# A decoder layer on one core: LN1's turned rows made by GpSimd, one transposition for a sequence's shifts, and a new order of all steps

## The chip, the cores and the metric

The kernel runs on one core of one Trainium2 chip. The metric is the device time of one execution in microseconds (us), lower is better. The time before is the median of three runs, 1078.32 us (1075.54 to 1079.03).

## What is computed

The input x is 32 sequences of 128 tokens by 256 features in f32; `ctx_1024` has the same shape. The layer has three parts, each with a residual (LN is layer normalisation without weights, eps 1e-5):

```
x = x + attn(LN1(x))        # causal linear attention, 16 heads of 16, phi = elu + 1, biases bq, bk, bv, bo
x = x + xattn(LN2(x), ctx)  # softmax attention on ctx, 16 heads of 16, Wq, Wk, Wv
x = x + ffn(LN3(x))         # silu(x w1) * (x w2), 256 -> 1024; gelu(h1), gelu(h2), 1024 -> 1024; w3, 1024 -> 256
```

The feed-forward weights are ternary, each with a scale per output.

## The kernel before, in words

**Tiles.** A group g (0 to 15) is two sequences, 256 tokens. Attention works on groups. The feed-forward net works on turns f (0 to 7) of two groups, 512 tokens. Activations that enter a matmul as f32r are split in two parts, the rounded value and the rest, and both are multiplied, so each feed-forward matrix costs two matmuls per 128x128 tile: 2816 matmuls of 128x512 in all, lines L1232 (`gate`), L1247 (`hidden`) and L1267 (`w3`).

**A group's attention, in the order of its data.** `load_x` brings x with tokens on partitions into `x_in` (L587). `ln1_stats` takes mean and variance on DVE (L861, L864) and the reciprocal deviation on POOL (L698, L701). `ln1` normalises in place on DVE (L867). `ln1T` turns the two sequences with four transpositions on PE (L1050, helper `turn`), and ACT (L756) and DVE (L871) take the rounded part and the rest out of PSUM into `xn1T`. Then q, k and v (L1074, L1079, L1089), the linear attention in 32-wide tiles (L1132 `scores`, L1105 `add_up`), the projection (L1182, L1185), LN2 (its transpositions are L1050 too, with `xb`), `xq`, and `max`: a first pass of the cross attention's scores, from which DVE takes each head's maximum (L981). `shift` writes minus the maximum as a bf16 pair into `nshift` (L990, L992), PE turns it with four bf16 transpositions per sequence (L1204), and ACT copies the 128x512 result to `shiftT` (L812). `x_scores` begins with matmuls of `onesb` and `shiftT` over 2 rows (L1125), which put the shift into PSUM, and adds the scores (L1132); `x_exp` (L816), `x_sums`, `x_div` and `x_turn` follow, then LN3, whose normalised rows are turned on PE (L1050, `xn`) into `hidden_b`. LN3's mean and deviation are stored to DRAM (`keep_stats`, L666), read back to all partitions (`load_stats`, L670), and POOL rebuilds the residual from them with four 128x256 operations a group (L722).

**Kept keys and values.** For groups 1 to 14 `xk` and `xv` are computed ahead of time, stored (`keep_k`, `keep_v`) and read back when their group comes (`load_k`, `load_v`).

**Weights.** `copy_weights` copies the 24 feed-forward weight tiles to `weights_scratch`, issued from ACT (L833). `ring` loads them tile by tile into a ring of four, 24 loads a turn (L613). `load_bits` and `low_bits` look at the low bits of the original weights.

**What sets the order.** At build time a planner (L62 to L391, with `LEAD`, `AT`, `needs` and `PATIENCE`) writes a fixed list of steps for each of the five engines. Each step has a due time (`PITCH` of 61.5 us times the group, plus an offset per step, plus a `LEAD` per engine and step), a booked duration, and the steps that it needs. On every engine the step with the earliest due time among those ready is put next. On PE, steps in 32-wide tiles wait until they are `PATIENCE` old or three of them have gathered, while feed-forward work fills in. The engines then run their lists strictly in order, with semaphores between them. SP's list holds nearly all DMAs; a wait on SP holds up every DMA behind it in the list. `x_in` is a single buffer: `load_x(g)` waits until PE has turned group g - 1.

## Time and profile before

| | |
|---|---|
| median of three runs | 1078.32 us |
| lowest, highest | 1075.54, 1079.03 us |
| span of the profiled execution | 1076.9 us |
| own time of the profiled execution, apart from its span | not given |
| TensorE busy, matmuls | 97%, 9898 |
| VectorE, ScalarE, GpSimd busy | 71%, 50%, 24% |
| mean granted TensorE clock | 0.996 |

PE is TensorE's matmuls, PEld its weight loads, DVE VectorE, ACT ScalarE, POOL GpSimd, SP the queue that issues DMAs. L12 is line 12 of the kernel before. A busy time unites overlapping instructions; the ends of matmuls are modelled. A stretch's row gives its limits and length, then for each engine the busy us with the count of instructions, then the granted clock as a share of full speed, the mean busy share of the 16 DMA engines, and GB/s. A group's row has the line, engine, operation, output and inputs, count, busy us and mean ns, and the engine's idle time before it with what ended it. A tile's row has ns min/median/max and the first and last start. A wait's row has total us, times, longest.

### The profile page before, as it was taken

To read this page: it belongs to the slowest core of one execution; us is meant where nothing else is said; L and a number is where in the kernel's file an instruction comes from. 1 tells how busy PE (TensorE), PEld (TensorE's weight loads), DVE (VectorE), ACT (ScalarE), POOL (GpSimd) and SP (SyncE) were. 2 spreads that over 40 slices of the span, in tenths; PEclk is the share of its full clock that TensorE was granted. 3 is DMA by queue.
4 is the path that set the end of the run, shared out by engine and by line. 5 is a ranking of instruction groups with operands and counts; after the bars stand their busy time and mean duration, and the time that the engine had idled before them with its cause. 6 is when DMAs were issued, how large, how long until landed. Compare 5 with 4: busy or idle time off the path is not lost.

```text
span 1076.9 us, 25119 instructions
## 1 busy us (share of the span) xinstructions
PE 1046.7 (97%) x9898; PEld 871.6 (81%) x9898; DVE 769.2 (71%) x1708; ACT 539.0 (50%) x857; POOL 259.7 (24%) x363
## 2 busy tenths in 40 slices
PE   7997899999999999999999999999999999999997
PEld 7987887888778888788887888888878788888886
DVE  6996798777987789888789676978587528433421
ACT  4452454646464644654555555473734364733431
POOL 4322345010531012601044101521026002400500
PEclk9999999999999999999999999999999999999999
DMA  5468887443644346534264434553364436545551
GB/s 163 168 215 276 270 269 245 138 138 113 198 146 138 104 109 206 164 106 149 85 230 142 149 109 137 174 166 109 109 218 149 166 105 206 184 148 178 181 169 65
DMA packets 76742, 174.86 MB, mean 162 GB/s; under 512 B 10960, under 2 KB 26448, under 8 KB 76624
## 3 DMA queue, kind: packets, MB, share of 16 engines
q1 hardware_dynamic: 73168, 161.70, 45.5%
q10 hardware_dynamic: 3456, 11.54, 3.7%
q8 instruction: 81, 1.33, 0.5%
q14 instruction: 37, 0.30, 0.1%
HBM read 145.38 MB, written 39.35 MB: 172 GB/s over the span
## 4 chain that ended last, share of the span: by engine, by line
PE 83%; DVE 8%; DMA 3%; issue 2%; POOL 1%; SPq 1%; ACT 0%; ACTq 0%; DVEq 0%; POOLq 0%
PE bank L1247 42%; PE bank L1132 7%; PE bank L1232 7%; PE bank L1267 5%; PE bank L1105 5%; PE bank L1074 5%; PE bank L1089 3%; PE bank L1079 2%; PE bank L1050 2%; DVE hidden_full L1012 1%; PE bank L1182 1%; DVE mx L981 1%; DMA stats_scratch<-mv 1%; DMA weight_ring<-weights_scratch 1%; PE bank L1125 1%
## 5 line engine op out<-in xcount | busy, mean ns | idle before, releaser
L1247 PE MATMUL bank<-hidden_a,weight_ring 128*128 128x512 f32 x1024 | 249.1, 395 | 0.0
L1247 PE MATMUL bank<-hidden_b,weight_ring 128*128 128x512 f32 x1024 | 247.9, 394 | 0.3 <-DVE inexact_flag L1037 0.3
L1247 PEld LDWEIGHTS bank<-hidden_b,weight_ring 128*128 128x128 f32 x1024 | 187.9, 188 | 39.8 <-issue 1.6
L1247 PEld LDWEIGHTS bank<-hidden_a,weight_ring 128*128 128x128 f32 x1024 | 187.6, 188 | 38.9 <-issue 0.8
L849 ACT ACTIVATE hidden_full<-bank,columns_sb 128x512 f32<-128x512 f32 x128 | 88.2, 689 | 187.9 <-PE bank L1247 187.2
L698 POOL TENSOR_TENSOR ve<-mv,eps 128x1 f32<-128x1 f32 (+1 forms) x80 | 18.5, 231 | 524.6 <-DVE mv L864 524.6
L1232 PE MATMUL bank<-hidden_b,weight_ring 128*128 128x512 f32 x512 | 122.9, 393 | 1.4 <-DMA weight_ring<-weights_scratch 1.0
L1232 PEld LDWEIGHTS bank<-hidden_b,weight_ring 128*128 128x128 f32 x512 | 94.3, 188 | 22.4 <-DMA weight_ring<-weights_scratch 1.8
L737 POOL TENSOR_TENSOR hidden_a<-hidden_full,hidden_a 128x512 fp32r<-128x512 f32 x64 | 83.8, 1313 | 104.2 <-ACT hidden_a L844 103.0
L1020 DVE TENSOR_TENSOR hidden_a<-hidden_full,hidden_a 128x512 fp32r<-128x512 f32 x64 | 43.8, 684 | 76.9 <-ACT hidden_a L855 76.7
L816 ACT ACTIVATE att_x<-bank 128x512 f32<-128x512 f32 x128 | 66.3, 603 | 48.0 <-PE bank L1132 47.9
L981 DVE TENSOR_REDUCE mx<-bank 128x4 f32<-128x512 f32 x128 | 80.4, 678 | 6.7 <-PE bank L1132 6.7
L960 DVE TENSOR_TENSOR att_l<-bank,cst 128x512 f32<-128x512 f32 x128 | 80.6, 679 | 6.2 <-PE bank L1132 6.0
L1020 DVE TENSOR_TENSOR hidden_b<-hidden_full,hidden_b 128x512 fp32r<-128x512 f32 x64 | 47.0, 736 | 51.0 <-ACT hidden_b L855 50.9
L901 DVE STREAM_TRANSPOSE by_token<-bank 128x512 f32<-128x512 f32 x64 | 45.6, 713 | 51.1 <-PE bank L1105 50.9
L839 ACT ACTIVATE hidden_full<-bank,s1h 128x512 f32<-128x512 f32 x64 | 44.0, 687 | 53.3 <-PE bank L1232 51.9
L1267 PE MATMUL bank<-hidden_a,weight_ring 128*128 128x512 f32 x256 | 65.9, 400 | 0.0
L722 POOL TENSOR_TENSOR residual<-residual,stats 128x256 f32<-128x256 f32 x64 | 59.0, 943 | 26.6 <-DMA stats<-stats_scratch 25.3
L844 ACT ACTIVATE hidden_a<-hidden_full 128x512 fp32r<-128x512 f32 x64 | 40.2, 630 | 31.3 <-DVE hidden_full L1015 31.1
L1267 PEld LDWEIGHTS bank<-hidden_a,weight_ring 128*128 128x128 f32 x256 | 45.8, 188 | 9.3 <-issue 0.4
L849 ACT ACT_TABLE_LOAD x39 | 50.0, 1283 | 0.7
L1015 DVE SCALAR_TENSOR_TENSOR hidden_full<-bank,s,hidden_full 128x512 f32<-128x512 f32 x64 | 48.1, 751 | 2.3
(135 smaller groups left out, 1715.5 us busy)
## 6 DMA issues: line engine op xcount, KB each, us to landing
weight_ring<-weights_scratch SPq DMA_DIRECT2D x160, 512.0 KB, 4.0
weights_scratch<-in_h ACTq DMA_DIRECT2D x16, 512.0 KB, 5.2
xn3T_scratch<-hidden_b SPq DMA_DIRECT2D x16, 512.0 KB, 4.2
weight_bits<-in_h SPq DMA_DIRECT2D x32, 256.0 KB, 4.2
weight_ring<-weights_scratch SPq DMA_DIRECT2D x32, 256.0 KB, 2.8
values_scratch<-hidden_full SPq DMA_DIRECT2D x14, 512.0 KB, 4.3
xv<-values_scratch SPq DMA_DIRECT2D x14, 512.0 KB, 4.9
x_in<-in_x SPq DMA_DIRECT2D x16, 256.0 KB, 2.8
```

The source lines that it names most:

```text
L722: last = eng.tensor_tensor(half[:, c], half[:, c], (sd, mean)[n], (ALU.mult, ALU.add)[n])
L737: eng.tensor_tensor(HA[:, 1, n, :], full[:, n % NFULL, :], HA[:, 0, n, :].bitcast(F32), ALU.subtract)\
L816: eng.activation(att_x[:, (NU * g + n) % NX, :, :], pbank("x_scores", g, n)[:, :].rearrange("p (j s) -> p j s", j=4), ACT.Exp, scale=SCALE ...
L849: eng.activation(full[:, (KH + n) % NFULL, :], pbank("hidden", g, n)[:, :], ACT.Gelu, scale=sc).then_inc(h_full, 1)
L960: eng.tensor_tensor(att_l[:, (NU * g + n) % NL, :, :], pbank("lin_scores", g, n)[:, :].rearrange("p (j s) -> p j s", j=4), causal.rearrang ...
L981: eng.tensor_reduce(mx[:, b, 4 * r:4 * r + 4], pbank("max", g, n)[:, :].rearrange("p (j t) -> p j t", j=4), AX.X, ALU.max).then_inc(max_do ...
L1020: eng.tensor_tensor(dst[:, 1, m, :], full[:, (KH + n) % NFULL, :], dst[:, 0, m, :].bitcast(F32), ALU.subtract)\
L1074: eng.matmul(pbank(step, g)[:, m * T:(m + 1) * T], w[:, i, c, m * P:(m + 1) * P], src[:, 0, c, :], start=(c + i == 0), stop=False)
L1132: mm = eng.matmul(pbank(step, g, 4 * b + r)[:, j * S:(j + 1) * S], stationary(rows, e, m, b), moving(rows, e, m, b), start=not shifted, st ...
L1232: mm = eng.matmul(pbank(step, g, n)[:, :], ring[:, n // 4, at_:at_ + P], HB[:, part, kk, :], start=(kk == 0 and part == 0), stop=(kk == C ...
L1247: mm = eng.matmul(pbank(step, g, n)[:, :], ring[:, slot, kk * P:(kk + 1) * P], src[:, part, kk, :], start=(kk == 0 and part == 0), stop=(k ...
L1267: mm = eng.matmul(pbank(step, g, c)[:, :], ring[:, slot, kk % 4 * P:(kk % 4 + 1) * P], HA[:, part, kk, :], start=(kk == 0 and part == 0), ...
```

## The change

1. **LN1 turned.** The host also passes `xT`, x with features on rows. For groups 1 to 15, `x_in` is loaded a second time after the statistics, with turned x (`load_xT`, 256 KB). Means and reciprocal deviations go to DRAM (`keep_stats1`) and come back spread over all partitions in two loads, means first (`load_stats1`, 128 KB each, into one buffer). POOL subtracts and multiplies in place, two 128x256 operations each (`xn1`). ACT and DVE read `xn1T`'s two parts from there. Group 0 stays as it was.
2. **Shifts.** `nshift` packs a sequence's 16 maxima in pairs into one 128x128 bf16 tile, 8 columns of each 32. PE turns it once. ACT writes it four times, each time with another mask as its scale, and the matmuls with ones go over 8 rows.
3. **Order.** New `LEAD` values and an `OFFSET` per group, `PATIENCE` 17.2, copies of the weights from 34.8 us on in steps of 8.76 us, `load_bits` in steps of 13.17 us, and tanh not counted as needing gelu's table. `load_x` waits for `xn1T` (DVE).

```diff
-    SPARE, PATIENCE, HOLD, MANY = 1, 18.5, 0, 3
+    SPARE, PATIENCE, HOLD, MANY = 1, 17.2, 0, 3
+    IN_TURNS = ("keep_xn", "keep_x2", "gate", "hidden", "w3", "tanh", "gated", "gate_round", "gate_rest", "gelu", "gelu_rest",
+                "out", "ring", "copy_weights", "split", "load_bits", "low_bits")
-            tasks[engine, step, g, n] = (rank + t + LEAD.get((engine, step), 0), took[engine])
+            lead = LEAD.get((engine, step), 0) + (0 if step in IN_TURNS else OFFSET[g])
+            tasks[engine, step, g, n] = (rank + t + lead, took[engine])
-    LEAD = {("gpsimd", "bias"): -14.1, ("gpsimd", "ctx"): -18.7, ("gpsimd", "gate_rest"): -4.2, ("gpsimd", "ln1_stats"): -3.1,
+    LEAD = {("gpsimd", "bias"): -14.9, ("gpsimd", "ctx"): -337.4, ("gpsimd", "gate_rest"): -294.4,
...
+    OFFSET = [-49.7, -36.8, 17.6, 63.5, -31.0, 123.6, -12.0, 61.9, 77.8, -63.7, -8.2, 64.3, 145.2, -46.8, -6.9, 115.5]
-        steady("ln1", vector=-12.6, took=dict(vector=.75))
-        steady("ln1T", tensor=-10.5, scalar=-8.63, vector=-7.75, took=dict(tensor=.4, scalar=.52, vector=.6))
+        if g == 0:
+            steady("ln1", vector=-12.6, took=dict(vector=.75))
+            steady("ln1T", tensor=-10.5, scalar=-8.63, vector=-7.75, took=dict(tensor=.4, scalar=.52, vector=.6))
+        else:
+            steady("load_xT", sync=-30, took=dict(sync=5))
+            steady("keep_stats1", sync=-25, took=dict(sync=2.2))
+            for n in range(2):
+                steady("load_stats1", n, sync=-24 + 4 * n, took=dict(sync=3))
+                steady("xn1", n, gpsimd=-20 + 4 * n, took=dict(gpsimd=1.75))
+            steady("ln1T", scalar=-8.63, vector=-7.75, took=dict(scalar=.52, vector=.6))
...
-    GELUS = ("tanh", "gelu")
+    GELUS = ("gelu",)
-    AT |= {("scalar", "copy_weights", j): 62 + 5.4 * j for j in range(NCH)}
-    AT |= {("sync", "load_bits", i, j): 150 + 17.5 * (NWB * i + j) for i in range(8) for j in range(NWB)}
+    AT |= {("scalar", "copy_weights", j): 34.8 + 8.76 * j for j in range(NCH)}
+    AT |= {("sync", "load_bits", i, j): 197.8 + 13.17 * (NWB * i + j) for i in range(8) for j in range(NWB)}
...
-                    wait_count(eng, xn1_turned, g)
+                    if g == 1:
+                        eng.wait_ge(xn1_turned, 1)
+                    elif g > 1:
+                        eng.wait_ge(xn1T_done, g)
...
+                    elif step == "load_xT":
+                        eng.wait_ge(LN1["mean_var"], GB * g + GB)
+                        eng.dma_start(x_t, xT.rearrange("(c p) t -> p c t", p=P)[:, :, T * g:T * g + T]).then_inc(xT_loaded, 16)
+                    elif step == "keep_stats1":
+                        eng.wait_ge(LN1["rstd"], g + 1)
+                        eng.wait_ge(mean1_copied, g)
+                        eng.dma_start(st1_d[g].rearrange("w p b -> p w b"), stats1_out[:, :, :]).then_inc(stats1_stored, 16)
+                    elif step == "load_stats1":
+                        eng.wait_ge(stats1_stored, 16 * g)
+                        if n == 1:
+                            eng.wait_ge(xn1_centred, g)
+                        elif g > 1:
+                            eng.wait_ge(xn1_made, g - 1)
+                        eng.dma_start(stats1[:, :, :].rearrange("p s b -> p (s b)"),
+                                      st1_d[g, n].rearrange("s b -> (s b)").partition_broadcast(P)).then_inc(stats1_loaded, 16)
...
+                        if g:
+                            eng.tensor_copy(stats1_out[:, 0, :], mv[:, 0, :, 0]).then_inc(mean1_copied, 1)
+                    elif step == "xn1":
+                        half = x_t.rearrange("p c (b s) -> p c b s", b=GB)
+                        mean_or_rstd = stats1[:, :, :].rearrange("p s b -> p b s")
+                        if n == 0:
+                            eng.wait_ge(xT_loaded, 16 * g)
+                        eng.wait_ge(stats1_loaded, 32 * g - 16 + 16 * n)
+                        for c in range(C):
+                            last = eng.tensor_tensor(half[:, c], half[:, c], mean_or_rstd, (ALU.subtract, ALU.mult)[n])
+                        last.then_inc((xn1_centred, xn1_made)[n], 1)
...
-                        eng.activation(xn1T[:, 0, :, :], halves(pbank(step, g)), ACT.Copy).then_inc(xn1T_hi, 1)
+                        eng.activation(xn1T[:, 0, :, :], halves(pbank(step, g)) if g == 0 else x_t, ACT.Copy).then_inc(xn1T_hi, 1)
...
-                        eng.activation(shiftT[:, n, :], pbank(step, g, n)[:, 0:2 * S].bitcast(BF16), ACT.Copy).then_inc(sh_done, 1)
+                        for j in range(4):
+                            last = eng.activation(shiftT[:, n, j * S:(j + 1) * S], pbank(step, g, n)[:, 0:S // 2].bitcast(BF16), ACT.Copy,
+                                                  scale=cst[:, 258 + j:259 + j])
+                        last.then_inc(sh_done, 1)
...
-                            eng.matmul(pbank(step, g, 4 * b + r)[:, :], onesb[32 * r:32 * r + 2, :], shiftT[32 * r:32 * r + 2, b, :],
+                            eng.matmul(pbank(step, g, 4 * b + r)[:, :], onesb[32 * r:32 * r + 8, :], shiftT[32 * r:32 * r + 8, b, :],
...
-                        for j in range(4):
-                            mm = eng.transpose(pbank(step, g, n)[:, j * S // 2:(j + 1) * S // 2].bitcast(BF16), nshift[:, n, j, :], identb[:, :])
-                        mm.then_inc(sh_psum, 1)
+                        eng.transpose(pbank(step, g, n)[:, 0:S // 2].bitcast(BF16), nshift[:, n, :], identb[:, :]).then_inc(sh_psum, 1)
```

The rest of the diff replaces every value of `LEAD`, adds the new steps to the table of needs, and adds buffers, semaphores and four mask columns in `constants`. Before it takes a group's statistics, DVE also waits until those of the group before are stored.

## Rows read from the trace of the kernel before

**Rows 1.** The page's head: span, busy time by engine

```profile
span 1076.9 us, 25119 instructions
...
PE 1046.7 (97%) x9898; PEld 871.6 (81%) x9898; DVE 769.2 (71%) x1708; ACT 539.0 (50%) x857; POOL 259.7 (24%) x363
```

**Rows 2.** Stretches: length; PE, PEld, DVE, ACT, POOL busy; clock; DMA share; GB/s

```profile
0.00:144.00 144.00, 126.82 (x1773) 118.05 (x1774) 115.70 (x295) 62.07 (x121) 44.13 (x67) 0.98 0.68 221
20.00:80.00 60.00, 57.19 (x827) 53.03 (x830) 54.06 (x136) 27.25 (x53) 18.32 (x26) 1.00 0.55 184
106.00:144.00 38.00, 35.26 (x511) 32.72 (x512) 30.87 (x80) 16.68 (x34) 11.06 (x18) 0.92 0.83 261
144.00:1004.00 860.00, 853.95 (x7837) 699.64 (x7836) 638.27 (x1391) 454.82 (x702) 204.69 (x285) 1.00 0.48 156
1004.00:1077.00 73.00, 65.89 (x291) 53.90 (x290) 15.27 (x24) 22.09 (x36) 10.88 (x12) 0.98 0.38 127
```

**Rows 3.** Waits of PE from 0 to 144 us: total us, times, longest

```profile
PE bank L1074 <- ACT hidden_full L806: 5.6, 2, 4.5
PE bank L1062 <- ACT identb L744: 5.5, 1, 5.5
```

**Rows 4.** Waits of SP's queue from 84 to 106 us, same columns

```profile
SPq L670 <- DMA stats_scratch<-mv: 9.9, 1, 9.9
```

**Rows 5.** Timeline of PE, 88 to 109 us: start, us, what

```profile
89.46 0.66 PE L1050 MATMUL bank<-cst,xn 128*128 128x128 f32 x4
89.87 0.71 PE L1074 MATMUL bank<-xn1T,wk 128*128 128x256 f32 x4
...
90.64 0.62 PE L1074 MATMUL bank<-xn1T,wk 128*128 128x256 f32 x4
...
95.96 0.40 PE L1204 MATMUL bank<-identb,nshift 128*128 128x128 bf16 x4 [0.33 <-DVE nshift L992]
96.17 0.72 PE L1182 MATMUL bank<-wo,oT 128*128 128x256 f32 x4
...
107.21 1.05 PE L1074 MATMUL bank<-ctxs,xwk 128*128 128x256 f32 x4
```

**Rows 6.** Groups by line: busy us, mean ns, idle before

```profile
L1247 PE MATMUL bank<-hidden_a,weight_ring 128*128 128x512 f32 x1024 | 249.1, 395 | 0.0
...
L1204 PE MATMUL bank<-identb,nshift 128*128 128x128 bf16 x128 | 12.9, 225 | 2.9 <-DVE nshift L992 2.9
...
L1050 PE MATMUL bank<-cst,x_in 128*128 128x128 f32 x64 | 10.2, 283 | 0.2 <-DVE x_in L867 0.2
```

**Rows 7.** Tile shiftT and line L746: ns min/median/max, first and last start

```profile
L1125 PE MATMUL bank<-shiftT,onesb x128: 371/385/462, 69.8 to 926.6; 2*128 2x512 bf16 x128
L812 ACT ACTIVATE shiftT<-bank x32: 580/597/625, 64.3 to 905.5; 128x512 bf16<-128x512 bf16 x32
...
L746 ACT ACTIVATE s1h<-columns_sb x1: 192/192/192, 5.3 to 5.3; 128x8 f32<-128x8 f32 x1
```

**Rows 8.** Tiles x_in and xn1T, the same columns

```profile
L867 DVE TENSOR_SCALAR x_in<-x_in,mv,rstd x32: 372/407/1362, 7.6 to 661.5; 128x256 f32<-128x256 f32 x32
...
L1074 PE MATMUL bank<-xn1T,wq x128: 276/278/387, 10.5 to 753.1; 128*128 128x256 f32 x128
...
L871 DVE TENSOR_TENSOR xn1T<-bank,xn1T x16: 659/687/693, 10.2 to 722.4; 128x512 fp32r<-128x512 f32 x16
```

**Rows 9.** Line L722 on GpSimd, the same columns

```profile
L722 POOL TENSOR_TENSOR residual<-residual,stats x64: 849/869/1416, 163.9 to 1019.6; 128x256 f32<-128x256 f32 x64
```

**Rows 10.** DMA to landing: tile x_in, then stats_scratch (stores and loads); timeline of SP

```profile
DMA to landing us min/median/max: 2.6/2.8/5.3
...
DMA to landing us min/median/max: 1.4/3.5/10.9
...
9.56 0.37 SPq L587 DMA_DIRECT2D x_in<-in_x  x1
```

**Rows 11.** Line L893 on DVE: ns min/median/max, first and last start

```profile
L893 DVE TENSOR_TENSOR o<-by_token,rec x64: 424/425/1536, 28.0 to 952.5; 128x256 f32<-128x256 f32 x64
```

More of the change, by code:

```diff
@@ L180, in needs @@
                 return [before, *([a("copy_weights", n // RING * RING + RING - 1)] if g == 0 else [])]
-            return {"load_x": [t("ln1T", g - 1)], "load_xb": [t("ln2T", g - 1)], "load_ctx": [p("ctx", g - 1)],
+            return {"load_x": [t("ln1T", 0) if g == 1 else v("ln1T", g - 1)], "load_xT": [v("ln1_stats", g)],
+                    "keep_stats1": [p("ln1_stats", g)], "load_stats1": [d("keep_stats1", g), p("xn1", g - (n == 0), 1 - n)], "load_xb": [t("ln2T", g - 1)], "load_ctx": [p("ctx", g - 1)],
                     "keep_k": [a("xk", g)], "keep_v": [a("xv", g)], "load_k": [d("keep_k", g), t("x_scores", g - 1, 1)],
@@ L189, in needs @@
                     "bias": [d("load_xb", g)], "gate_rest": [a("gate_round", g, n)],
+                    "xn1": [d("load_xT", g), d("load_stats1", g, n)],
                     "res": [a("xn3T", g), d("load_stats", g), p("gate_rest", f, KH - 1)]}[step]
@@ L195, in needs @@
                     + ([d("keep_v", KEPT[-1])] if g == 0 else [])
-            return {"ln1T": [t(step, g), t("v", g - 1)], "split": [], "ctx": [d("load_ctx", g), t("xk", g - 1), t("xv", g - 1)],
+            return {"ln1T": [t(step, g) if g == 0 else p("xn1", g, 1), t("v", g - 1)], "split": [], "ctx": [d("load_ctx", g), t("xk", g - 1), t("xv", g - 1)],
                     "q": [t(step, g), v("k_heads", g - 1)], "k": [t(step, g), v("q", g)], "xq": [t(step, g), t("x_scores", g - 1, 1)],
@@ L205, in needs @@
         if engine == "vector":
-            return {"ln1_stats": [d("load_x", g)], "ln1": [p("ln1_stats", g)], "split": [a(step, g)], "ln1T": [a(step, g)],
+            return {"ln1_stats": [d("load_x", g), d("keep_stats1", g - 1)], "ln1": [p("ln1_stats", g)], "split": [a(step, g)], "ln1T": [a(step, g)],
                     "q": [a(step, g), t("lin_scores", g - 1, 1)], "k": [a(step, g)], "k_heads": [v("k", g), t("lin_scores", g - 1, 1)],
@@ L454, in decoder_layer_program @@
             stats3 = sb("stats3", [P, S, GB, 2])
+            stats1 = sb("stats1", [P, S, GB])
+            stats1_out = sb("stats1_out", [P, 2, GB])
+            x_t = x_in[:, :, :].rearrange("p b d -> p (b d)").rearrange("p (c t) -> p c t", c=C)
             ve, rstd = sb("ve", [P, 3, GB]), sb("rstd", [P, 3, GB])
@@ L860, in mean_var @@
                 def mean_var(ln, which, src, g, b):
+                    if which == 0 and b == 0 and g > 1:
+                        eng.wait_ge(stats1_stored, 16 * (g - 1))
                     eng.bn_stats(stats[:, which, b, :], src).then_inc(ln["stats"], 1)
@@ L929, in _ @@
                         eng.wait_ge(xn1T_hi, g + 1)
-                        rest(xn1T, pbank(step, g)[:, :]).then_inc(xn1T_done, 1)
+                        rest(xn1T, pbank(step, g)[:, :] if g == 0 else x_t.rearrange("p c t -> p (c t)")).then_inc(xn1T_done, 1)
                     elif step == "ln2T":
@@ L988, in _ @@
                         m_ = mx[:, n, :].rearrange("p (r j) -> p r j", r=4)
[L989 removed]
+                        hi, lo = (nshift[:, n, :].rearrange("p (r j a) -> p a r j", r=4, a=2)[:, a, :, 0:4] for a in range(2))
                         eng.tensor_scalar(hi, m_, -1.0, None, ALU.mult).then_inc(sh_hi, 1)
@@ L1478, in constants @@
     import numpy as np
-    c = np.zeros((128, 258), np.float32)
+    c = np.zeros((128, 262), np.float32)
     c[:, 0:128] = np.eye(128)
     c[:, 128:256] = np.triu(np.ones((128, 128)))
+    for j in range(4):
+        c[:, 258 + j] = np.arange(128) % 32 // 2 == j
     c[:, 256], c[:, 257] = np.arange(128) // 16 % 2 == 0, np.arange(128) // 16 % 2 == 1
@@ L1508 @@
         "x": np.ascontiguousarray(a["x"]),
+        "xT": turned(a["x"].reshape(B * S, D)),
         "ctxT": turned(a["ctx_1024"].reshape(B * S, D)),
```

66 lines of the change are left out of this document (37 added, 29 removed).

## Prediction

> **What bounds the kernel now.** I read the page's head first [rows 1]: TensorE (PE) is busy 97% of the 1076.9 us, VectorE (DVE) 71%, ScalarE (ACT) 50%, GpSimd (POOL) 24%. An average hides stages, so the second view is the busy time by stretch [rows 2]. It shows three stages. In the first 144 us only attention work of the first groups runs, and PE is idle for 144.00 - 126.82 = 17.2 us. From 144 to 1004 us attention and feed-forward are mixed, and PE is idle for 6.1 us of 860. The last 73 us are feed-forward alone, with 7.1 us idle, most of it the last eviction and store. So in the long middle stage an instruction taken from PE shortens the run by its own length, and a better order has almost nothing to win there. What an order can win lies in the first stage. PE's waits there [rows 3] are led by 5.5 us for the first constant, and by 5.6 us behind ACT, 4.5 of them at once. That one is an event with a cause: PE waited for ACT, ACT for a load of the other sequence's input, and SP could only issue that load after it had waited 9.9 us for the store of LN3's statistics to land [rows 4]. Behind it the granted clock is 0.92 in the mean of 106 to 144 us [rows 2]; if the lower level is half, that is 2 x 0.08 x 38 = 6.1 us at 1.2 GHz, and four matmuls of L1074 take 1.05 us there where 0.62 is usual [rows 5]. That costs another 3.0 us. The event is worth 4.5 + 3.0 = 7.5 us, and the whole first stage, without the first constant, at most 17.2 - 5.5 + 3.0 = 14.7 us.
>
> **The change, part by part.**
>
> *LN1's transpositions leave PE.* 15 of 16 groups lose four f32 transpositions of L1050. Busy time says 10.2 us for 64 of them, so 9.6 us for 60 [rows 6]. But matmuls overlap, so I take the distance between starts: from L1050 at 89.46 to the next line at 89.87, 0.41 us for four [rows 5]. 15 x 0.41 = **6.2 us**.
>
> *The shifts' transpositions.* 32 times four bf16 transpositions become 32 times one. Busy time says three quarters of 12.9 us, 9.7 us [rows 6]. Start to start, four take 96.17 - 95.96 = 0.21 us [rows 5]; a quarter stays, so 0.16 x 32 = **5.0 us** go. Together 11.2 us leave PE by distances, against 19.3 us by busy time. A busy piece of 0.66 us at 89.46 has its successor 0.41 us later, which is why I take the first. The page "Perfetto Trace Analysis" of the Trainium skill, section "Identifying the Most-Contended Engine", calls matmul busy time a bad metric because matmuls are pipelined. By busy time the sum would be 8 us lower; that is part of rival A.
>
> *The rank-2 matmuls of L1125 become rank 8.* 128 of them. No row shows eight rows of 512 columns. The nearest are two rows, 385 ns in the median [rows 7], and 128 rows, 395 ns in the mean [rows 6]: 64 times as many rows add 10 ns, at most 1.3 us for all 128. I take 0.
>
> *Four masked copies for one on ACT.* The copy of 128x512 takes 597 ns, one of 128x8 takes 192 ns [rows 7]. A line through the two gives 0.8 ns per column, so 128 columns take about 290 ns and four of them 1.2 us, 0.6 us more for each of 32 sequences: 19 us on an engine that is idle half of the time. The planner still books 0.55 us for the step. It lies on the way from the maxima to `x_scores`. The first copy begins at 64.3 us and the matmul that reads it at 69.8, the last at 905.5 and 926.6 [rows 7], so 5 to 21 us lie between, and 0.6 us more is hidden: 0. Without that cover it would be up to 0.6 x 32 = 19 us. PATIENCE, which makes such steps wait, falls only from 18.5 to 17.2.
>
> *LN1 through GpSimd.* Per group DVE loses two normalisations of 0.41 us [rows 8], 15 x 0.81 = 12 us off an engine that is not the bound over the span. POOL gets four 128x256 operations; L722 does that shape in 869 ns [rows 9], so 3.5 us a group and 52 us for 15, besides a small copy each. POOL goes from 260 to about 315 us, under 30%. ACT and DVE now read `xn1T`'s source from SBUF and not from PSUM, about the same time, and one PSUM bank per group is not taken: 0. The chain of a group from the load of x to `xn1T` was 2.8 us of load [rows 10], 1.15 statistics and 1.0 POOL as the planner books them, 0.8 DVE, 0.4 PE, 0.6 ACT, 0.7 DVE: 7.4 us. It becomes 2.8 load, 1.15 and 1.2 for the statistics, 3.5 store of the statistics, 3.5 load of the means (the load of turned x beside it), 1.7 centring, 3.5 load of the second row, which needs the buffer of the first, 1.7 scaling, and 0.6 and 0.7: 20.4 us [rows 8 to 10]. In the middle stage that is free: the last group's `xn1T` is made at 722.4 us and first read at 753.1 [rows 8], 30 us early, and groups come about every 61.5 us (PITCH). In the first stage it must fit too. Group 1's x is only loaded from 9.56 us on [rows 10], so its q can come at 30 us at the earliest. What PE has in its place are `xk` and `xv` of 14 kept groups, which the planner books at 2.9 us each. I count 0 to 3 us as lost here, and take 1.
>
> *SP's queue.* Each of 15 groups adds four issues on SP of about 0.4 us, some 24 us of a queue that mostly waits for ring slots, and 512 KB of transfers, 7.7 MB in all. The middle stage alone moves 156 GB/s x 860 us = 134 MB [rows 2], so this is under 6% more. But `load_stats1` waits on SP until `keep_stats1` has landed, and behind it stand ring loads, `load_ctx` and `load_k`. The planner books 2.2 us for that landing. A transfer of statistics took 3.5 us in the median and 10.9 at worst [rows 10]; the worst fell in the first stage, whose DMA share is 0.68 against 0.48 later [rows 2]. The weights' copies go from one per 5.4 us, from 62 us on, to one per 8.76 us from 34.8 on, which thins that stretch. `load_x` of the next group now waits for `xn1T` on DVE, also on SP. Cost: between 0 and rival B's; I take 0 beyond the item below.
>
> *The order.* All due times move, and tanh no longer counts as needing gelu's table. ACT is off the path, so the latter gives nothing by itself. An order can give back at most the 14.7 us of the first stage, and at worst lose more there. I take half of the event of 7.5 us, rounded to 4.
>
> *Sum:* 1076.9 - 11.2 - 4 + 1 = 1062.7 us against the profiled execution's span (no other time of that execution is shown). The median of the three runs, 1078.3, is 1.4 us above it, so **1064 us**.
>
> **The rivals.**
>
> *A. Much faster.* The event goes entirely (4 us more) and the longer chain costs nothing (1 us), or the removal is worth its busy time (8 us more). That is 1056 to 1059 us, and 1051 with all of it. For it: both lie on PE. Against: groups 1 and 2 now wait for a chain nearly three times as long, and the distances speak against the busy time. Chance 0.20.
>
> *B. Stores of statistics block SP in the first stage; slower.* The one such store that took 10.9 us cost PE 7.5 us. `keep_stats1` with `load_stats1` behind it runs for groups 1 to 4 or 5 in about that stretch. With the old event gone, two such stores give 1078.3 - 11.2 - 7.5 + 15.0 = 1075 us, no change; it decides from the third on, 1082 us, and four give 1090. For it: the code waits on SP, and the planner books too little. Against: the weights' copies are spread, and SP's wait may be put after the landing. Chance of slower 0.14.
>
> *C. VectorE, slowed by GpSimd, bounds the first stage; no change.* DVE is busy 54.06 of 60 us from 20 to 80 us [rows 2]. An operation of L893 takes 425 ns in the median and 1536 at most [rows 11]; the 1.1 us more is about the length of one wide POOL operation, which takes 849 to 1416 ns [rows 9]. Each group's xn1 is 3.5 us of such work. If DVE stood still for all of it, four groups would lose 14 us less 3 us of removed DVE work: 1064 + 11 = 1075 us. The skill's "GPSIMD Engine Reference", section "Key points", says that the two engines share their SBUF interfaces and that VectorE is about twice as fast at elementwise work; the long L893 agrees with the first. By that rule the move would be wrong wherever DVE nearly bounds. Against: most DVE operations read PSUM or one operand, and the POOL steps are few. Together with B at two stores, the chance of no change is 0.10.
>
> **How the numbers follow.** Forecast 0.56, A 0.20, no change 0.10, slower 0.14. A measurement of this kernel tells 0.3% (3.2 us) from no change, so faster is below 1075.1 us. Faster 0.56 + 0.20 = 0.76, same 0.10, slower 0.14. The forecast's own range is 1058 to 1070. The range reaches down into A and up over the no-change cases: 1053 to 1079.
>
> **What would show it.** L1050 with `x_in` x4 and L1204 x32 in place of 64 and 128; ACT copies for `shiftT` x128 with 280 to 310 ns; POOL near 315 us; PE busy 15 to 20 us lower while PE stays busy about 99% of the stretch from 144 us to the last 73. The forecast is wrong if PE's idle time of the first 144 us is above 20 us, or the middle stage shows more than 10 us of it. B shows as SP waiting long for the store of `stats1` and PE idle behind it. C shows as L893 well above 425 ns in the median and as PE waiting for DVE.

## The result, and the profile after

The changed kernel takes 1091.32 us in the median of four runs (1086.52 to 1093.47), against 1078.67 us before (four runs as well): ratio 1.0122, 95% interval 1.0098 to 1.0147. It is slower by 12.7 us, 11 to 16 by the interval, outside the range of 1053 to 1079 and on the other side. The profiled execution is the fastest of the four. The page's head:

```profile
span 1084.7 us, 25062 instructions
...
PE 1038.9 (96%) x9742; PEld 862.7 (80%) x9742; DVE 759.5 (70%) x1678; ACT 550.9 (51%) x949; POOL 310.4 (29%) x438
```

PE's busy time is 7.8 us lower than in [rows 1], and yet the span is 7.8 us longer. The stretches of the changed kernel (length, then busy us per engine, granted clock, DMA share, GB/s):

```profile
0.00:240.00 240.00, 209.34 (x2579) 184.39 (x2580) 181.61 (x437) 110.37 (x217) 90.42 (x134) 0.96 0.69 207
240.00:1004.00 764.00, 756.00 (x6841) 618.04 (x6840) 557.73 (x1212) 413.99 (x690) 204.42 (x290) 1.00 0.50 160
...
0.00:144.00 144.00, 118.95 (x1673) 109.46 (x1674) 105.06 (x263) 62.50 (x129) 54.00 (x84) 0.95 0.73 216
144.00:1004.00 860.00, 846.39 (x7747) 692.97 (x7746) 634.29 (x1385) 461.86 (x778) 240.84 (x340) 1.00 0.52 164
```

and the same view of the kernel before:

```profile
0.00:240.00 240.00, 222.71 (x2717) 196.34 (x2718) 193.60 (x476) 113.66 (x202) 73.99 (x109) 0.99 0.64 210
240.00:1004.00 764.00, 758.06 (x6892) 621.34 (x6891) 560.37 (x1210) 403.24 (x620) 174.84 (x243) 1.00 0.46 151
```

In the first 240 us PE is idle for 30.7 us where it was 17.3, and the mean clock is 0.96 where it was 0.99, so work in it is slower too. From 240 to 1004 us idle time is 8.0 against 5.9 us. In the stretches of the forecast it is 25.1 us up to 144 us (17.2 before) and 13.6 us from 144 to 1004 us (6.1 before), so both signs that I had named for a wrong forecast occurred: more than 20 us in the first, more than 10 us in the second. The first `w3` matmul of turn 0 dates the loss. Before, then after (ns min/median/max, first and last start):

```profile
L1267 PE MATMUL bank<-hidden_a,weight_ring x256: 387/392/504, 259.6 to 1069.8; 128*128 128x512 f32 x128
```

```profile
L1326 PE MATMUL bank<-hidden_a,weight_ring x256: 387/390/500, 276.5 to 1077.5; 128*128 128x512 f32 x128
```

It starts at 276.5 us, 16.9 us late. From there to the end of the span the changed kernel needs 808.2 us, the one before 817.3: 9.1 us less. From that matmul on PE runs 6793 matmuls in place of 6968. Of the 175 fewer, 102 are transpositions of the change (LN1's of nine groups and the shifts' of 22 sequences, worth 7.2 us by the forecast's distances), and 73 are small matmuls, mostly 32-wide ones, that the new order has put ahead of it. So a gain of the size forecast is there, a part of the 9.1 us is moved work, and the first quarter loses nearly twice as much. The other three runs took 3.4 to 7.0 us longer than the profiled one, with a mean clock of 0.984 to 0.986 against 0.990. By an estimate, 0.005 less over 1090 us is 11 us more at the lower of the two levels (1.2 GHz, not 2.4), 5.5 us of time, which is about that distance.

The operations of the change, by tile (same columns), and the transposition once more by line (busy us, mean ns, idle before):

```profile
L1264 PE MATMUL bank<-identb,nshift x32: 219/230/230, 64.9 to 895.3; 128*128 128x128 bf16 x32
...
L869 ACT ACTIVATE shiftT<-bank,cst x128: 360/377/443, 65.6 to 896.5; 128x128 bf16<-128x128 bf16 x128
...
L1186 PE MATMUL bank<-shiftT,onesb x128: 371/384/385, 74.2 to 914.3; 8*128 8x512 bf16 x128
...
L758 POOL TENSOR_TENSOR x_in<-x_in,stats x60: 729/743/1199, 24.6 to 741.2; 128x256 f32<-128x256 f32 x60
...
L1111 PE MATMUL bank<-cst,x_in x4: 272/273/331, 8.3 to 8.7; 128*128 128x128 f32 x4
```

```profile
L1264 PE MATMUL bank<-identb,nshift 128*128 128x128 bf16 x32 | 7.2, 229 | 1.7 <-DVE nshift L1053 1.7
```

Counts are as forecast. A masked copy takes 377 ns, not 290. The rank-8 matmul takes 384 ns, as the rank-2 one did. GpSimd's operation takes 743 ns in the median, less than L722's 869.

SP's waits (whole span), GpSimd's wait at xn1, and PE's longest of the first 240 us, each with total us, times, longest; then the DMA issues of the statistics (count, KB, median us to landing):

```profile
SPq L681 <- DMA stats_scratch<-stats_out: 57.0, 14, 8.4
SPq L678 <- POOL x_in L758: 46.8, 14, 5.4
```

```profile
POOL x_in L758 <- DMA stats<-stats_scratch: 116.6, 27, 11.0
```

```profile
PE bank L1135 <- ACT xn1T L812: 6.3, 2, 4.8
PE bank L1193 <- ACT xqf L836: 6.1, 2, 4.7
...
PE bank L1140 <- POOL ctxs L779: 3.8, 3, 2.6
```

```profile
stats<-stats_scratch SPq DMA_DIRECT2D x30, 128.0 KB, 4.1
...
stats_scratch<-stats_out SPq DMA_DIRECT2D x15, 2.0 KB, 4.9
```

GpSimd stands 116.6 us at xn1 until a load of LN1's statistics has landed. Its steps behind it stand too. That wait has no counterpart before. (Not all of it is lost time: GpSimd waits less for other things, 323 us for DVE's statistics where it was 525.) The chain of work that ended at 62 us shows the round trip of groups 1 and 2:

```profile
9.03 0.37 SPq L614
...
17.55 2.80 DMA stats_scratch<-stats_out
20.37 4.12 DMA stats<-stats_scratch
...
24.62 1.44 POOL x_in L758 x2
26.13 3.27 DMA stats<-stats_scratch
...
29.47 1.45 POOL x_in L758 x2
30.94 0.64 ACT xn1T L812
31.62 0.74 PE bank L1135 x4
...
41.85 4.42 DMA stats_scratch<-stats_out
...
46.67 0.42 SPq L690
47.15 7.28 DMA ctx_in<-in_ctxT
54.45 0.64 ACT ctxs L820
...
55.16 1.52 POOL ctxs L779
56.68 1.25 POOL xb L785
57.93 1.60 POOL x_in L758 x2
```

Group 1's chain is all there: store, load, centre, load, scale, then ACT and q at 31.62 us, 22.6 us after x was asked for; I had counted 20.4. PE waited for it for only 1.5 us. In group 2 the store takes 4.42 us, and SP stands still for it, with a load of the statistics, a store of `xv` (L690, 46.67 us) and `load_ctx` behind it. `load_ctx` goes out at 47.15 us and lands 7.3 us later, so `ctxs` on GpSimd only runs at 55.16, and the scaling stands behind it until 57.93.

Two rows of PE's timeline show the two ways in which the round trip reaches PE. First, GpSimd's standing delays other groups' work. PE's row, then GpSimd's, then ACT's:

```profile
133.54 0.50 PE L1140 MATMUL bank<-ctxs,xwk 128*128 128x256 f32 x2 [2.56 <-POOL ctxs L779]
...
130.83 1.42 POOL L758 TENSOR_TENSOR x_in<-x_in,stats 128x256 f32<-128x256 f32 x2 [6.86 <-DMA stats<-stats_scratch]
132.21 1.28 POOL L779 TENSOR_TENSOR ctxs<-ctx_in,ctxs 128x512 fp32r<-128x512 f32 x1
...
127.61 0.63 ACT L820 ACTIVATE ctxs<-ctx_in 128x512 fp32r<-128x512 f32 x1 [3.00 <-DMA ctx_in<-in_ctxT]
```

ACT's part of `ctxs` was ready at 128.2 us, but GpSimd stood 6.9 us for statistics and came to `ctxs` at 132.2, and PE waited 2.6 us for it. Second, the chain alone is too long. PE, then the store of that group's statistics:

```profile
206.28 1.18 PE L1135 MATMUL bank<-xn1T,wq 128*128 128x256 f32 x4 [4.76 <-ACT xn1T L812]
...
186.38 7.52 DMA stats_scratch<-stats_out
```

Two loads follow that store as in group 1, and q comes 19.9 us after it was issued. PE has no `xk` or `xv` work between 153 and 207 us, so nothing of that kind fills this gap, which lies well behind the first 144 us.

### The profile page after: what moved, and what is told of

Its sections match the earlier page's. It is cut to its first block, busy times and chain, and to the rows that moved or that the text cites. A ratio compares the mean times of both kernels' runs of the same rounds, so it can differ in the third digit from the quotient of the medians.

```text
span 1084.7 us, 25062 instructions
## 1 busy us (share of the span) xinstructions
PE 1038.9 (96%) x9742; PEld 862.7 (80%) x9742; DVE 759.5 (70%) x1678; ACT 550.9 (51%) x949; POOL 310.4 (29%) x438
## 4 chain that ended last, share of the span: by engine, by line
PE 65%; DMA 14%; DVE 11%; POOL 4%; issue 3%; SPq 1%; ACT 1%; ACTq 0%; DVEq 0%; POOLq 0%
PE bank L1306 34%; PE bank L1291 8%; PE bank L1193 5%; DMA stats_scratch<-stats_out 5%; PE bank L1326 5%; DMA stats<-stats_scratch 4%; PE bank L1166 3%; PE bank L1135 3%; DVE mx L1042 2%; PE bank L1150 2%; POOL x_in L758 2%; PE bank L1140 1%; DMA ctx_in<-in_ctxT 1%; DMA weight_bits<-in_w 1%; PE bank L1111 1%
## 5 line engine op out<-in xcount | busy, mean ns | idle before, releaser
L1306 PE MATMUL bank<-hidden_b,weight_ring 128*128 128x512 f32 x1024 | 249.9, 396 | 0.5 <-DVE inexact_flag L1098 0.3
L1306 PE MATMUL bank<-hidden_a,weight_ring 128*128 128x512 f32 x1024 | 246.7, 394 | 0.0
L1291 PE MATMUL bank<-hidden_b,weight_ring 128*128 128x512 f32 x512 | 124.7, 395 | 1.5 <-DMA weight_ring<-weights_scratch 1.5
L740 POOL TENSOR_TENSOR ve<-mv,eps 128x1 f32<-128x1 f32 (+1 forms) x80 | 21.7, 271 | 323.5 <-DVE mv L925 323.3
L758 POOL TENSOR_TENSOR x_in<-x_in,stats 128x256 f32<-128x256 f32 x60 | 45.9, 785 | 116.6 <-DMA stats<-stats_scratch 116.6
L1326 PE MATMUL bank<-hidden_a,weight_ring 128*128 128x512 f32 x256 | 63.7, 398 | 0.0
```

Of the source, the lines that this page charges most:

```text
L758: last = eng.tensor_tensor(half[:, c], half[:, c], mean_or_rstd, (ALU.subtract, ALU.mult)[n])
L1291: mm = eng.matmul(pbank(step, g, n)[:, :], ring[:, n // 4, at_:at_ + P], HB[:, part, kk, :], start=(kk == 0 and part == 0), stop=(kk == C ...
L1306: mm = eng.matmul(pbank(step, g, n)[:, :], ring[:, slot, kk * P:(kk + 1) * P], src[:, part, kk, :], start=(kk == 0 and part == 0), stop=(k ...
L1326: mm = eng.matmul(pbank(step, g, c)[:, :], ring[:, slot, kk % 4 * P:(kk % 4 + 1) * P], HA[:, part, kk, :], start=(kk == 0 and part == 0), ...
```

## The experiments

Theories after the result; S and O were written down first, L and G after the first four runs. **S/L**: the round trip of LN1's statistics (store, two loads, and who waits for them) costs, by holding up a queue (S: SP's) or by the chain's length (L). **O**: the new list of steps costs by itself. **G**: GpSimd's added work does. All ratios are against the kernel before on the same chip.

| run | median us | ratio, 95% interval |
|---|---|---|
| shift_only | 1076.00 | 0.9974, 0.9952 to 0.9996 |
| both_parts_old_order | 1137.29 | 1.0507, 1.0443 to 1.0571 |
| new_order_alone | 1090.78 | 1.0105, 1.0070 to 1.0141 |
| no_wait_for_store | 1082.99 | 1.0034, 1.0012 to 1.0056 |
| constant_stats | 1070.22 | 0.9913, 0.9882 to 0.9945 |
| constant_stats_one_column | 1069.59 | 0.9907, 0.9871 to 0.9942 |
| turned_from_5 | 1088.87 | 1.0096, 1.0064 to 1.0127 |
| turned_from_8 | 1077.34 | 0.9977, 0.9958 to 0.9996 |
| second_load_gone | 1088.94 | 1.0095, 1.0062 to 1.0127 |
| loads_by_gpsimd | 1126.23 | 1.0418, 1.0377 to 1.0458 |
| sp_waits_only | 1074.53 | 0.9964, 0.9942 to 0.9986 |
| pool_waits_for_store | 1071.38 | 0.9928, 0.9900 to 0.9955 |
| act_waits_for_loads | 1081.01 | 1.0017, 0.9991 to 1.0042 |
| robust_order_from_1 | 1102.59 | 1.0235, 1.0195 to 1.0274 |
| robust_order_from_8 | 1075.82 | 0.9969, 0.9949 to 0.9990 |
| robust_order_from_16 | 1081.96 | 1.0036, 1.0019 to 1.0054 |
| const_and_transpositions | 1076.80 | 0.9988, 0.9971 to 1.0005 |
| constant_stats_again | 1072.61 | 0.9942, 0.9922 to 0.9962 |

### The parts and the order apart

`shift_only` is the kernel before with the hunks of the shifts alone (`nshift`, `onesb` and the masks with them):

```diff
-                        for j in range(4):
-                            mm = eng.transpose(pbank(step, g, n)[:, j * S // 2:(j + 1) * S // 2].bitcast(BF16), nshift[:, n, j, :], identb[:, :])
...
+                        eng.transpose(pbank(step, g, n)[:, 0:S // 2].bitcast(BF16), nshift[:, n, :], identb[:, :]).then_inc(sh_psum, 1)
```

> The kernel before with the shifts' part alone: one transposition, four masked copies, 8 rows of ones; LN1 and the list of steps exactly as before. If distances between starts are the right measure, PE loses 5.0 us and the time is 1078 - 5 = about 1073 us; by busy time it would be 1069. If the masked copies (377 ns each in the changed kernel, 0.9 us more per sequence than one copy) hold up x_scores, it is 1078 or more.

1076.0 us, 0.4 to 5.2 us faster. On PE's timeline the one transposition has its successor 0.10 us later here, where four had it after 0.21 us [rows 5]. Over the whole traces the median distance is 0.04 us for one (31 places) and 0.21 us for four (32 places):

```profile
94.67 0.23 PE L1206 MATMUL bank<-identb,nshift 128*128 128x128 bf16 x1 [0.27 <-DVE nshift L995]
94.77 0.71 PE L1185 MATMUL bank<-wo,oT 128*128 128x256 f32 x4
```

The interval holds the 5.0 us of the forecast at its edge, and not the 9.7 us of busy time. PE waits for `shiftT` 0.7 us in this trace, once. A cost of the masked copies of a few us, which would fill the gap to 5.0, is not excluded.

`both_parts_old_order` puts the due times of before into the changed kernel:

```diff
-    LEAD = (those of the change), OFFSET = [-49.7, -36.8, ...]
+    LEAD = (those of before, none for the new steps), OFFSET = [0.0] * 16
-    PATIENCE 17.2, GELUS = ("gelu",), copies from 34.8 us on
+    PATIENCE 18.5, GELUS = ("tanh", "gelu"), copies from 62 us on
```

> Both parts of the change with the due times, PATIENCE and copy times of before (no lead for the new steps, no offsets per group). Theory S (SP blocked by the store of LN1's statistics, whatever the order): 1085 to 1092, SP waits of about 50 us for stats_scratch remain and PE is idle 25 us in the first 144 us. Theory O (the new due times are what costs): 1067 to 1072.

`new_order_alone` is the reverse: the kernel before with the change's `LEAD`, `OFFSET`, `PATIENCE`, `GELUS` and copy times.

> The kernel before with the due times, offsets, PATIENCE, tanh rule and copy times of the change, neither of its parts. Theory O: slower than before by 10 us or more, 1088 to 1098. Theory S: within 5 us of before, 1073 to 1083.

1137 us is worse than either theory said, and 1091 us without either part fits O. But a planner given other steps writes another list, so these two runs measure two lists that nobody would use. What they do show is that a list can move the time by about the 13 us in question: `new_order_alone` is 12 us slower than before, without either part. From here on most runs keep the changed kernel's list step for step.

### The round trip, with the list unchanged

`no_wait_for_store`:

```diff
                     elif step == "load_stats1":
-                        eng.wait_ge(stats1_stored, 16 * g)
...
-                                      st1_d[g, n].rearrange("s b -> (s b)").partition_broadcast(P)).then_inc(stats1_loaded, 16)
+                                      x[g, n].partition_broadcast(P)).then_inc(stats1_loaded, 16)
```

> The changed kernel with its list of steps unchanged; the two loads of LN1's statistics read rows of x in place of the stored statistics, same size, and so do not wait on SP for the store to land (the store stays). LN1 of groups 1 to 15 is then computed with other numbers. Theory S: SP loses its 57 us of waits for that store, PE's idle time of the first 144 us falls from 25 to below 15 us, and the time is 1074 to 1080. Theory O: 1088 or more.

1083.0 us: 8 us of it, but PE's idle time in the profiled first 144 us stayed at 24.7 us, where the changed kernel has 25.1, so theory S as I had put it fell short. GpSimd still stood 91.9 us at xn1 there, for the loads.

`constant_stats` and `constant_stats_one_column`:

```diff
                     elif step == "load_stats1":
-                        (waits and load)
+                        pass
...
-                        mean_or_rstd = stats1[:, :, :].rearrange("p s b -> p b s")
+                        mean_or_rstd = bob[:, :].rearrange("p (s b) -> p b s", b=GB)
...
```

So GpSimd works with the constant row of the bias `bo` and waits for no load; LN1 of groups 1 to 15 comes out with other numbers. In the second run the operands are `half[:, c, :, 0:1]` and `mean_or_rstd[:, :, 0:1]`.

> The changed kernel with its list of steps unchanged, but the two loads of LN1's statistics for groups 1 to 15 are gone from SP, and GpSimd takes one constant row (bo, already in SBUF) as mean and as reciprocal deviation. LN1 of these groups is so computed with other numbers. Theory L (the whole round trip of the statistics, store, two loads and their waits on SP, is what costs): PE idle in the first 240 us falls from 31 to 18 us or less and the time is 1070 to 1078. If it stays above 1082, the list of steps itself costs, whatever SP waits for.

> As the run beside it, and GpSimd's 60 wide operations of xn1 work on one column in place of 128 (LN1 of groups 1 to 15 is not normalised). Theory G (GpSimd's length and its sharing with VectorE cost): at least 4 us less than the run beside it. Without it: within 2 us.

1070.2 us, 21 us below the changed kernel and 6 to 13 below the one before. So the list itself is good, once the statistics do not travel: O falls for the changed kernel. The stretches and GpSimd's waits of `constant_stats`:

```profile
0.00:240.00 240.00, 218.61 (x2715) 192.56 (x2716) 187.89 (x455) 119.76 (x234) 93.28 (x140) 0.98 0.70 210
240.00:1004.00 764.00, 759.24 (x6769) 621.93 (x6770) 563.20 (x1204) 411.43 (x685) 214.84 (x294) 1.00 0.50 157
...
POOL ctxs L776 <- ACT ctxs L817: 55.5, 14, 8.7
...
POOL x_in L755 <- DMA x_in<-in_xT: 6.1, 4, 3.4
```

PE's idle time in the first 240 us is 21.4 us, 9.3 less than in the changed kernel (I had expected 18 or less), and 4.8 us from 240 to 1004. GpSimd stands 6 us at xn1, where it stood 117. One column in place of 128 takes 0.6 us more off, with runs that spread over 7 us: theory G falls, and rival C, which asked for 11 us, with it. The changed kernel's trace says the same: the operation that C feared for (L893, now L954) takes 426 ns in the median, 1179 at most.

`second_load_gone` keeps the first load and its wait, and drops the second:

```diff
-                    elif step == "load_stats1":
+                    elif step == "load_stats1" and n == 1:
+                        pass
+                    elif step == "load_stats1":
```

> The changed kernel with its list of steps unchanged; the load of the means stays with its wait for the store, the second load (reciprocal deviations, which waits on SP until the centring has freed the buffer) is gone, and GpSimd scales by the constant row bo. LN1 of groups 1 to 15 is so scaled with other numbers. If the second load with its 47 us of waits on SP makes up most of the 21 us that the round trip costs: 1073 to 1079. If the store's landing makes it up: 1084 or more.

`loads_by_gpsimd` moves both loads to GpSimd's list, each ahead of its operation:

```diff
+                            eng.wait_ge(stats1_stored, 16 * g)
+                        else:
+                            eng.wait_ge(xn1_centred, g)
...
+                        eng.dma_start(stats1[:, :, :].rearrange("p s b -> p (s b)"),
+                                      st1_d[g, n].rearrange("s b -> (s b)").partition_broadcast(P)).then_inc(stats1_loaded, 16)
                         eng.wait_ge(stats1_loaded, 32 * g - 16 + 16 * n)
```

> The changed kernel with its list of steps unchanged, complete; both loads of LN1's statistics are issued by GpSimd, its only reader, right ahead of the operation that needs them, and SP waits for neither the store's landing nor the centring. If it was SP's blocked queue that cost (and not the latency of the chain itself): 1070 to 1078, below the kernel before. If the latency of the chain costs: 1085 or more, with PE behind ACT xn1T.

The first gives 1088.9, only 2 us better, which its interval does not tell from nothing: with the store and a load left, the second is not the sore point, and the single effects (2 and 8 us) do not add up to 21. The second is the worst of the fixed lists, 1126 us. SP waits for no statistics of LN1 there, and GpSimd's waits and PE's say why:

```profile
POOL x_in L759 <- DMA stats<-stats_scratch: 119.3, 30, 6.3
...
POOL stats L755 <- issue: 35.3, 11, 6.4
...
PE bank L1136 <- ACT xn1T L813: 9.6, 3, 5.3
PE bank L1141 <- POOL ctxs L780: 9.4, 5, 4.2
```

GpSimd now stands 119 us for loads, and 35 us more ahead of issuing them, where its list has the wait for the store's landing, and PE waits for `xn1T` and for `ctxs`, which is GpSimd's too. An issue also takes GpSimd 0.55 to 0.75 us in the first 60 us, and SP 0.33. So a queue that has other groups' work should not stand for a round trip. Three more runs on the base of `constant_stats` put single waits back:

```diff
 sp_waits_only, on SP at the places of the loads:
+                        eng.wait_ge(stats1_stored, 16 * g)    # n = 0
+                        eng.wait_ge(xn1_centred, g)           # n = 1
 pool_waits_for_store, on GpSimd ahead of centring:
+                            eng.wait_ge(stats1_stored, 16 * g)
 act_waits_for_loads, SP with its waits and loads, on ACT ahead of xn1T:
+                            eng.wait_ge(stats1_loaded, 32 * g)
```

> As constant_stats (no loads of LN1's statistics, GpSimd works with the constant row bo), but SP stands at the places of the two loads and waits there as in the changed kernel: for the store's landing, and for the centring. GpSimd waits for no load, so the chain of LN1 stays short and only SP's queue is held up. If SP's held-up queue is what costs: 1082 to 1090. If it is the length of the chain through the loads: 1070 to 1074.

> As constant_stats, but GpSimd waits for the store's landing before it centres; SP waits for nothing. The chain grows by the landing (4.4 us in the median for the tile) and GpSimd's own queue is held up. If the chain's length or GpSimd's queue costs: 1076 or more. If only SP's queue does: 1070 to 1073.

> The changed kernel with its list of steps unchanged. SP issues the store and both loads of LN1's statistics with all its waits (the second load after the first has landed), but GpSimd works with the constant row bo and waits for no load; ACT waits for both loads before it copies xn1T. LN1 of groups 1 to 15 is computed with other numbers. The chain up to xn1T is as long as in the changed kernel less about 3 us. If the chain's length costs: 1084 to 1092. If GpSimd's held-up queue costs: 1072 to 1080.

They build a ladder (the runs come from five chips, so a step of 1 or 2 us says nothing): 1070 to 1073 without the round trip (two measurements), 1071.4 with the store's landing on GpSimd, 1074.5 with SP's waits, 1081.0 with the whole chain but ACT as the one that waits, 1091.3 in the changed kernel, where GpSimd waits. `act_waits_for_loads` in the first 240 us, and GpSimd's wait there:

```profile
0.00:240.00 240.00, 213.28 (x2591) 187.71 (x2592) 184.50 (x443) 112.29 (x221) 93.13 (x137) 0.96 0.70 209
...
POOL x_in L760 <- DMA x_in<-in_xT: 5.7, 4, 3.5
```

So of the 21 us (19 from the second measurement) some 2 to 4 are SP's queue, some 6 the loads in the chain, and some 10 come with GpSimd's standing. The last two are not cleanly apart: with ACT as the waiting one, centring and scaling run ahead, and the chain is about 3 us shorter. `sp_waits_only` and `act_waits_for_loads` lie just outside the ranges that a single cause was given. `pool_waits_for_store` has the value written down for a cost of SP's queue only: GpSimd stood 26.1 us for the store there, at no cost that shows. So a wait on GpSimd is not dear by itself, and the single effects depend on what else stands: the same landing awaited on SP costs 2 to 4 us with nothing else in the way, and 8 us in the changed kernel (`no_wait_for_store`).

`const_and_transpositions` puts PE's work back into `constant_stats`, ahead of q of groups 1 to 15:

```diff
+                            wait_pbank(eng, step, g)
+                            for n in range(4):
+                                eng.transpose(pbank(step, g)[:, n * S:(n + 1) * S], ident, ident)
```

> As constant_stats, and ahead of q of groups 1 to 15 PE makes four f32 transpositions of the unit matrix into q's bank, whose results are overwritten. If the distance between starts was the right measure: 5 to 6.2 us more than constant_stats (1070.2), so 1075 to 1077. By busy time it would be 1080. If PE had slack there: 1070 to 1072.

> constant_stats once more, on the same chip as the run beside it, so that the two compare directly: 1068 to 1072.

1076.8 against 1072.6 us: 4.2 us by the medians, 5.0 by the two ratios, 2 to 8 by their intervals. That is the size of the forecast's 6.2 us and not of the 9.6 us of busy time. (The median distance over the 15 places in the trace before is 0.36 us, not 0.41, which gives 5.4.) PE has no slack that hides them.

### Versions that should beat both

`turned_from_5` and `turned_from_8` keep PE's transpositions for the first 5 and 8 groups, with the list made from the due times of before and longer bookings:

```diff
-        if g == 0:
+        if g < K1:
             steady("ln1", vector=-12.6, took=dict(vector=.75))
...
-            steady("keep_stats1", sync=-25, took=dict(sync=2.2))
+            steady("keep_stats1", sync=-25, took=dict(sync=5))
```

> Due times, PATIENCE and copy times of the kernel before; the shifts' part; LN1 by GpSimd only from group 5 on, the first five groups keep PE's transpositions; the planner books 5 us for the store of LN1's statistics, 4.1 for a load of them and 1.35 for the four masked copies. Removed from PE: 11 x 0.41 + 32 x 0.16 = 9.6 us. Theory L with its place in the first stage: 1068 to 1074, below both kernels. If the round trip costs in the middle stage too: 1080 or more.

> As the run beside it with group 8 as the first by GpSimd. Removed from PE: 8 x 0.41 + 5.1 = 8.4 us. Theory L: 1069 to 1075. If the order of steps moves the time by more than the parts do, the two runs differ by over 4 us.

`turned_from_5` missed its range by 15 us: 1088.9. Its first operation of xn1 starts at 131.7 us, so nearly all of the round trips are behind the first stage. PE's idle time up to 144 us is 17.9 us, as before, but 10.0 us from 240 to 640 us against 4.3, of which 6.7 between 400 and 480. PE's longest waits in that piece are for DVE (2.7 and 2.3 us), so whether the round trip or the new list is to blame stays open. At least it does not bear out that the longer chain is free in the middle stage under any list.

The `robust_order` runs choose the due times anew, so that the list also holds if steps take longer than booked. The number in the name is again the first group whose rows GpSimd makes (16: none, so the shifts' part alone). Against `turned_from_8`:

```diff
-    LEAD = (those of before)
+    LEAD = (others for every step)
-    K1 = 8
+    K1 = 1 (8, 16)
```

> The full change (groups 1 to 15 by GpSimd, shifts), with bookings of 5, 4.1 and 1.35 us for the store, a load and the masked copies, the copy times and PATIENCE of before, and due times chosen so that the list also holds when the bookings of all engines but PE are stretched at random by up to 25% (DMAs 60%). If too short bookings made the changed kernel slow: 1068 to 1080. If the round trip costs in any order: 1085 or more.

> The same with LN1 by GpSimd from group 8 on. The first stage keeps PE's transpositions, so nothing of the round trip stands in it; 8.4 us leave PE. 1064 to 1074, below both kernels and at or below the shifts' part alone (1076).

> The shifts' part alone, with due times chosen in the same way. Tells the order's share: 1070 to 1076. If it is as low as the run with LN1 from group 8 on, the moved transpositions give nothing.

From group 1 on, the third list, with longer bookings, still gives 1102.6 us: longer bookings do not mend it, and none of the three orders tried carries the round trip in the first stage. From group 8 on, the loss is gone (1077.3 and 1075.8), though both runs lie 2 us above the ranges expected, and the 3.3 us of the moved transpositions do not show beside `shift_only`. GpSimd's wait and the stretches of `robust_order_from_8`:

```profile
POOL x_in L737 <- DMA stats<-stats_scratch: 59.8, 14, 9.4
...
0.00:240.00 240.00, 223.21 (x2729) 195.90 (x2733) 196.49 (x481) 118.27 (x227) 73.52 (x109) 0.99 0.63 210
240.00:1004.00 764.00, 752.50 (x6757) 614.50 (x6753) 556.58 (x1189) 412.19 (x688) 203.35 (x284) 1.00 0.48 156
```

The first 240 us are as good as before, and the middle has 11.5 us idle in place of 5.9. The shifts' part with another list gives 1082.0 (1070 to 1076 expected) in place of 1076.0, so a list alone moves 6 us, more than that part gives. The two best complete versions, `shift_only` and `robust_order_from_8`, are equal, and 0.3% faster than the kernel before. None found is clearly better.

## Why the prediction was wrong

- **Three stages, PE the bound.** Right. From 276 us on the kernel gained 9.1 us, of which the sum had 7.2 and moved work gave a part, and PE's added transpositions cost their length in `const_and_transpositions`.
- **LN1's and the shifts' transpositions, 6.2 + 5.0 us by distances between starts.** Right in size, if rather high: 4 to 5 us for the first, and 2.6 us (0.4 to 5.2) for the second. The sign I had named, PE's busy time 15 to 20 us lower, was wrong: it fell by 7.8 us. The two groups' own rows fell by 15.2 us (23.1 to 7.9), since a transposition that stands alone still shows 229 ns where four together showed 0.40 us. Much of that lay over the busy time of neighbours and so never was in the total, and the other groups' rows rose by 2.6 us. The Trainium skill ("Perfetto Trace Analysis", "Identifying the Most-Contended Engine") says that matmul busy time misleads on how near TensorE is to its limit, because matmuls are pipelined. The trace agrees that it misleads, also on what a removal is worth.
- **Rank 8, masked copies.** Rank 8 costs nothing (384 against 385 ns). A copy took 377 ns and not 290, so four are 1.5 us; PE waited for `shiftT` 0.3 us, once, in the changed kernel, so nearly all of it was hidden, as forecast.
- **"LN1 through GpSimd ... I count 0 to 3 us as lost here, and take 1."** This step failed. The chain's length was right (20.4 forecast, 22.6 in group 1). What I made of it was wrong. I let PE fill the time with `xk` and `xv` and did not ask what these need: `ctx` is loaded through SP and split by GpSimd, the two queues in which the round trip stands. The cover was behind the same queues as the stall (2.6 us of PE's time at 133.5 us), and at 201.5 us, when the `xk` and `xv` of the kept groups had been made, a chain with a store of 7.5 us, where I had counted 3.5, cost PE 4.8 us by its length alone. What is queued behind a waiting instruction I had named for SP only. GpSimd's wait at xn1, 116.6 us in all, is in no term of the sum. Where the sum had 1 us, the whole round trip measured 19 to 21 us (`constant_stats` and its repetition against the changed kernel), some 16 of them beyond SP's queue when that is measured alone.
- **"SP's queue ... I take 0."** Measured alone, 2 to 4 us; with the rest of the round trip in place, taking the wait for the store off SP (and the landing out of the chain) gave back 8. Low.
- **The order gives back 4 us.** The event behind the store of LN3's statistics is gone (SP waits 1.9 us for such a store in all, not 14.5), but others took its place: idle time in the first 240 us rose from 17.3 to 30.7 us. Without the round trip the same list had 21.4, so it gave back nothing there.
- **Rival B** had the right sign and stage and nearly the right size (1082 for three stores, 1090 for four), with a chance of 0.14. Its mechanism was only part of it: blocked SP is the smaller share. **Rival C** is refuted by the one-column run, **A** did not occur. In place of the sum: 1078.3 - 8 (the parts and the list, `constant_stats`) + 21 (round trip) = 1091; both terms come from the same runs, so this splits the result and does not test it.

## What to carry to other kernels

A chain that goes through DRAM and back should be read as what each waiting engine has behind the wait, and not only as a latency against the slack of its own consumer: in this kernel an engine that waited for a landing held up other groups' work in its list. When filler work is named as the cover of a stall, follow the filler's own inputs: if they pass the stalled queues, there is no cover. To see what a suspected wait is worth, keep the list of steps and feed the reader a constant: a run that makes a new list measures the list.

## What the hardware showed that I had not expected

- A lone bf16 transposition shows 219 to 230 ns of PE busy, and its successor starts 0.04 us later in the median (31 places in `shift_only`); four in a row show 0.40 us, with 0.21 us to the successor. Four f32 ones show 0.66 us for 0.36.
- The median landing of a 2 KB store of statistics was 4.9 us for LN1's 15 (2.5 us for LN3's 16 in the same trace), and a transfer of 128 KB of the same statistics took 4.1.
- Stalls in the first stage came with a lower clock: PE's idle time in the first 240 us rose by 13.4 us, and the mean clock fell from 0.99 to 0.96, which is an estimated 7 us of work more (0.03 of 240). The runs of one and the same kernel spread from 1086.5 to 1093.5 us with mean clocks of 0.990 to 0.984.
